# Attention with a bias behind the softmax, on one core: the preparation ahead of round 0, and the form in which the key and query parts are stored, are rebuilt

## The chip, the cores and the metric

The kernel runs on 1 core of a Trainium2 chip. The metric is the device time of one execution in microseconds (us). TensorE (PE) multiplies and loads weights (PEld), VectorE (DVE), ScalarE (ACT) and GpSimd (POOL) do the elementwise work, and SyncE (SP) issues most of the DMAs.

## The reference, cut to what matters

```python
def _L0_attn_ref(x, Wq, Wk, Wv, rel_table, gamma, beta):
    b, s, e = x.shape                       # 4, 512, 128; 16 heads of 8
    q = split_heads(x @ Wq); k = split_heads(x @ Wk); v = split_heads(x @ Wv)
    attn = softmax(jnp.einsum('bhqd,bhkd->bhqk', q, k) * e ** -0.5)
    bias = rel_table[clip(r[None, :] - r[:, None] + s - 1, 0, 2 * s - 2)]
    attn = attn + bias.reshape(-1).reshape(h, s, s)[None]
    out = jnp.einsum('bhqk,bhkd->bhqd', attn, v)      # then heads side by side
    return (out - mean) / sqrt(var + 1e-3) * gamma + beta

x = _layernorm(x + _L0_attn_ref(...))
x = _layernorm(x + _L0_ffn_ref(...))        # product keys: top 4 of 32 experts per token
```

All in float32. The bias does not depend on the batch and is added behind the softmax, so its share of the output is bias @ v.

## The kernel before

The kernel is written engine by engine, with every wait on a semaphore by hand; the order of the lines of an engine's block is its order of work. There are B = 4 batches of S = 512 tokens, H = 16 heads of D = 8 columns, in G = 4 groups of J = 4 heads, and C = 4 pieces of 128 tokens.

**Parts.** A product of float32 numbers is made in bf16: each of q and k is split into three bf16 parts (high, middle, low) whose sum is the number. Every part of q has to meet every part of k, so the stack of a head has TERMS = 72 rows (8 columns times 9 pairs of parts), and one matmul over 72 rows (96 with zeros) gives the exact scores. `parts` holds the three parts in SBUF. `write_parts` (L359) writes them to the DRAM tensor `stack_dram` [batch, q or k, head, 72, 512], each part three times; for batch 0 the first group of heads goes first. `load_slice` (L324) loads one group's 72 rows of four heads into `q_stack` and `k_stack`, 288 KB each.

**Preparation, before round 0.** `prep(b)` on PE (L1105) turns x of batch b, makes q, k and v of it. ACT (L632 to L650) copies the turned x (`x_t`), the high parts, the middle parts and v. DVE makes what is left of q and k (L819) and the low parts of batch 0 (L824); POOL makes the other low parts (L500). The bias needs the table `rel_win`, turned to `rel_t`; bias @ v of groups 0 and 1 is one product (L1321, kept by `bias_spread`), that of groups 2 and 3 is made in pieces (L1344) that ACT copies (`bias_copy`), PE turns and ACT keeps (`bias_keep`).

**Maxima.** The softmax needs the maximum of each row of scores before the exponential. PE makes the scores of 128 queries against 512 keys in one of two banks of `sm_ps`, DVE reduces them to a column of `neg_max` (L838). Maxima run 7 units ahead of the scores that use them, so 24 "early" maxima (`early_maxima`) stand between the pieces of the preparation. After the 16 maxima of a group POOL splits the column block (`split_shift`), PE turns it, ACT copies it (`shift_copy`, 0.3 us) and SP loads it into three rows of `q_stack` (`load_shift`, L335; 3 x 16 pieces of 256 bytes, from 48 partitions).

**Rounds.** Round t (0 to 4) has 16 units. A unit makes scores for four heads (`scores`), four maxima (five in the first four units of round 0), the products with v (`values`), and ACT takes four exponentials (L713). From round 1 on the feed-forward layer of the batch before lies between them. The first `scores` of round 0 waits for the shift rows of group 0 (L1168) and for all of the bias (L1362).

**SP's queue** is in order: each DMA is issued when those before it have been, and a wait blocks all behind it. `load_slice` of (t, g) waits until round t - 1 is done with group g.

## Time and profile before

| | |
|---|---|
| median of 3 runs | 312.98 us (312.96 to 313.03) |
| the profiled execution | 312.77 us, span 311.0 us |
| busy: PE, DVE, ACT, POOL | 91%, 75%, 64%, 40% of the span |
| round 0 begins (first scores) | 41.40 us from the span's start |
| moved over HBM | 12.18 MB read, 10.52 MB written |

The profile shows one execution, of 312.77 us; 1.77 us of it lie around the span. Times of instructions count from the span's start. A share of DMA is the mean busy share of 16 DMA engines: 0.75 is 12 engines at work. "A <- B" behind a row names what the engine waited for.

### The profile page before, as it was taken

What the parts mean: (1) busy time and instruction counts of PE and PEld (TensorE: products, weight loads), DVE (VectorE), ACT (ScalarE), POOL (GpSimd) and SP (SyncE); (2) the same over time, 40 slices, a digit from 0 to 9 for tenths busy, and PEclk for the clock granted to TensorE, in tenths of its full rate; (3) what the DMA queues carried; (4) which work ended last, traced back from release to release, by engine and by line L of the source; (5) the groups of instructions that cost most, each with busy time, mean ns of one, the idle gap of its engine ahead of it and who ended that gap; (6) DMA issues with size and microseconds to landing.
All of it is one profiled execution on the core that took longest, in us unless ns stands there. A gap on an engine that the chain in (4) does not pass through costs nothing.

```text
span 311.0 us, 9808 instructions
## 1 busy us (share of the span) xinstructions
PE 283.6 (91%) x4087; PEld 131.2 (42%) x4087; DVE 231.8 (75%) x516; ACT 199.1 (64%) x392; POOL 125.8 (40%) x209
## 2 busy tenths in 40 slices
PE   4878988999998989999999999999999999889991
PEld 2545232333333333343455543434555433284390
DVE  4547788988889969987798699977986952167673
ACT  2575276777676767789865667898665689902500
POOL 8393511101102751127556312297563033943133
PEclk9999999999999999999999999999999999999997
DMA  6475597359432303000403020006000000100002
GB/s 171 103 235 175 144 322 122 80 207 308 179 99 57 81 4 78 6 2 17 140 4 78 4 78 5 3 8 184 4 2 6 2 5 1 36 4 2 0 6 62
DMA packets 28265, 23.48 MB, mean 76 GB/s; under 512 B 6542, under 2 KB 26686, under 8 KB 28222
## 3 DMA queue, kind: packets, MB, share of 16 engines
q1 hardware_dynamic: 27950, 22.73, 25.9%
q8 instruction: 32, 0.52, 0.7%
q10 hardware_dynamic: 272, 0.13, 0.1%
q14 instruction: 11, 0.09, 0.1%
HBM read 12.18 MB, written 10.52 MB: 73 GB/s over the span
## 4 chain that ended last, share of the span: by engine, by line
PE 62%; DVE 15%; POOL 8%; ACT 7%; issue 4%; DMA 3%; SPq 1%; POOLq 0%; DVEq 0%
PE sm_ps L1139 13%; PE st_ps L1139 11%; PE ov_ps L1189 11%; DVE neg_max L838 9%; PE si_ps L1139 6%; PE mi_ps L1139 5%; ACT probs L713 3%; PE mi_ps L1195 2%; PE st_ps L1412 2%; POOL rstd L466 2%; PE sm_ps L1150 2%; DVE stats L877 2%; ACT w_rows L624 1%; DMA k_stack<-stack_dram 1%; PE si_ps L1213 1%
## 5 line engine op out<-in xcount | busy, mean ns | idle before, releaser
L838 DVE TENSOR_REDUCE neg_max<-sm_ps 128x1 f32<-128x512 f32 x256 | 166.0, 685 | 37.1 <-PE sm_ps L1139 30.9
L713 ACT ACTIVATE probs<-st_ps 128x512 f32<-128x512 f32 x256 | 138.3, 613 | 41.7 <-PE st_ps L1139 41.7
L1139 PE MATMUL sm_ps<-k_stack,q_stack 96*32 96x512 bf16 x928 | 91.6, 383 | 4.5 <-DVE neg_max L838 3.9
L1139 PE MATMUL st_ps<-q_stack,k_stack 128*32 128x512 bf16 x1024 | 89.0, 380 | 1.3 <-ACT bias_v L624 0.7
L1189 PE MATMUL ov_ps<-probs,v_cur 128*32 128x512 f32 x512 | 66.5, 592 | 0.0
L1139 PEld LDWEIGHTS sm_ps<-k_stack,q_stack 96*32 96x32 bf16 x928 | 24.7, 94 | 64.6 <-DVE neg_max L838 52.7
L480 POOL TENSOR_TENSOR hid<-hid,w_rows 128x512 f32<-128x512 f32 x26 | 32.9, 1281 | 36.1 <-ACT w_rows L624 36.0
L1139 PEld LDWEIGHTS st_ps<-q_stack,k_stack 128*32 128x32 bf16 x1024 | 27.5, 96 | 34.8 <-ACT probs L713 16.0
L901 DVE SCALAR_TENSOR_TENSOR hid<-tanh_sb,mi_ps 128x512 f32<-128x512 f32 x24 | 16.3, 680 | 12.0 <-ACT tanh_sb L750 12.0
L1139 PE MATMUL mi_ps<-x_t,down_sb 128*32 128x512 f32 x192 | 25.0, 592 | 0.0
L1139 PE MATMUL si_ps<-up_sb,hid 128*32 128x128 f32 x768 | 24.0, 272 | 0.0
L1139 PEld LDWEIGHTS si_ps<-up_sb,hid 128*32 128x32 f32 x768 | 21.3, 110 | 5.0 <-issue 3.5
L436 POOL CAST shift_parts<-neg_max 128x16 bf16<-128x16 f32 x16 | 3.1, 195 | 46.8 <-DVE neg_max L838 45.1
L750 ACT ACTIVATE tanh_sb<-mi_ps 128x512 f32<-128x512 f32 x24 | 14.9, 620 | 8.1 <-PE mi_ps L1139 8.1
L1189 PEld LDWEIGHTS ov_ps<-probs,v_cur 128*32 128x32 f32 x512 | 16.2, 110 | 8.5
L624 ACT ACTIVATE w_rows<-si_ps 128x512 f32<-128x512 f32 x24 | 15.6, 648 | 0.7 <-PE si_ps L1139 0.6
L452 POOL COPY v_cur<-v_all 128x128 f32<-128x128 f32 x16 | 4.5, 291 | 23.7 <-PE ov_ps L1189 23.7
L624 ACT ACTIVATE x_t<-mi_ps 128x512 f32<-128x512 f32 x4 | 2.4, 597 | 13.5 <-PE mi_ps L1195 13.5
L1139 PE MATMUL si_ps<-w_t,spread 96*32 96x512 bf16 x96 | 9.4, 382 | 1.5 <-ACT w_rows L624 1.5
L1150 PE MATMUL sm_ps<-k_stack,q_stack 96*128 96x512 bf16 x24 | 8.9, 385 | 2.0 <-DMA k_stack<-stack_dram 1.5
L461 POOL TENSOR_SCALAR veps<-mv 128x4 f32<-128x4 f32 x8 | 1.9, 235 | 18.4 <-DVE mv L886 18.4
L466 POOL TENSOR_TENSOR rstd<-veps,minus_half 128x4 f32<-128x4 f32 x8 | 8.3, 1038 | 0.2
(166 smaller groups left out, 297.3 us busy)
## 6 DMA issues: line engine op xcount, KB each, us to landing
stack_dram<-parts SPq DMA_DIRECT2D x18, 384.0 KB, 4.5
q_stack<-stack_dram SPq DMA_DIRECT2D x16, 288.0 KB
k_stack<-stack_dram SPq DMA_DIRECT2D x16, 288.0 KB
stack_dram<-parts SPq DMA_DIRECT2D x6, 288.0 KB, 4.4
x_sb<-L_attn_x SPq DMA_DIRECT2D x4, 256.0 KB, 3.9
out<-y_out SPq DMA_DIRECT2D x3, 256.0 KB, 2.3
stack_dram<-parts SPq DMA_DIRECT2D x6, 96.0 KB, 2.1
down_sb<-L_ffn_values_down SPq DMA_DIRECT2D x1, 512.0 KB, 9.0
```

Of the source, the lines that this page charges most:

```text
L466: nc.gpsimd.tensor_tensor(scale[:], v[:], minus_half[:], ALU.pow).then_inc(done, 1)
L480: nc.gpsimd.tensor_tensor(hid[:, j], hid[:, j], w_rows[:, j], ALU.mult).then_inc(weighed, 1)
L624: return nc.scalar.activation(dst, src, ACT.Copy, scale=scale)
L713: nc.scalar.activation(probs[:, u % 2, j, :], st_ps[:, score_bank(u * J + j), :], ACT.Exp, scale=SCORE_SCALE).then_inc(probs_ready, 1)
L750: nc.scalar.activation(tanh_sb[:, j % 3, :], mi_ps[:], ACT.Tanh, scale=0.5).then_inc(act_step, 1)
L838: nc.vector.tensor_reduce(neg_max[:, g % 2, col:col + 1], sm_ps[:, c % 2, :], AX.X, ALU.max, negate=True).then_inc(max_ready, 1)
L877: i = nc.vector.bn_stats(into[:, c, :], src[:, c, :])
L901: nc.vector.scalar_tensor_tensor(out=hid[:, j], in0=tanh_sb[:, j % 3, :], scalar=1.0, in1=mi_ps[:], op0=ALU.add, op1=ALU.mult).then_inc(hi ...
L1139: i = nc.tensor.matmul(dst[n * TILE:(n + 1) * TILE], weights[:, n * TILE:(n + 1) * TILE], moving, **flags)
L1150: return nc.tensor.matmul(dst, weights, moving, **flags)
L1189: i = nc.tensor.matmul(ov_ps[j * TILE:(j + 1) * TILE, :], v_cur[:, kc, g * J + j, :], probs[:, u % 2, j, :], start=(g % 2 == 0 and kc == 0 ...
L1195: return nc.tensor.transpose(dst, src, idn)
```

## The change

- The parts are stored once: `parts_dram` [batch, q or k, 24 rows, head, 512]. The load makes the 72 rows of them: its source pattern has a dimension with stride 0 and count 3. For q that dimension is the inner one (24 rows, each three times), for k it is the outer one (three times 24 rows). A row of four heads is one piece of 4 KB. A batch's write is 6 DMAs of 128 KB in place of 6 of 384 KB; batch 0's first group goes out part by part as the parts are made, and its DMAs have the four heads as outer dimension.
- x of all batches is loaded first; the weights are loaded from ACT's queue. PE turns x of batches 0 and 1 first, then those of 2 and 3. The turned x lie in `hid`, v is copied by DVE.
- The bias pieces use other PSUM banks and `tiled` maxima (four products of 32 columns) between them.
- k of the last batch is made after maximum 18, its q after maximum 23; their parts are made within round 0, at units 0 and 3.
- The load of `rel_win`, `hasher` and `keys` moves behind batch 0's first writes.

```diff
-        stack_dram = nc.dram_tensor("stack_dram", [B, 2, H, D * PARTS * PARTS, S], BF16, kind="Internal").ap()
+        parts_dram = nc.dram_tensor("parts_dram", [B, 2, PARTS * D, H, S], BF16, kind="Internal").ap()
...
+        def turned_bank(b):
+
+            return [st_ps[:, 0, :], ov_ps[:, :], sm_ps[:, 0, :], sm_ps[:, 1, :]][b]
+
+        def qk_bank(b, a):
+
+            return [(st_ps[:, 1, :], st_ps[:, 2, :]), (mi_ps[:, :], si_ps[:, :])][b % 2][a]
...
@@ -328,9 +341,9 @@
                     sp.wait_ge(scores_ready, (t - 1) * (J * U) + J * C * (g + 1))
                     apart(sp)
                 for a, stack in enumerate((q_stack, k_stack)):
-                    src = stack_dram[t, a, g * J:(g + 1) * J]
-                    sp.dma_start(stack[0:TERMS, g * J:(g + 1) * J, :], src.rearrange("h r s -> r h s")) \
-                      .then_inc(stack_loaded[g], 16)
+                    rows = [[H * S, PARTS * D], [0, PARTS]] if a == 0 else [[0, PARTS], [H * S, PARTS * D]]
+                    src = bass.AP(parts_dram.tensor, (t * 2 + a) * PARTS * D * H * S + g * J * S, rows + [[1, J * S]])
...
 
             sp.sem_inc(y_stored, 1)
 
+            def load_x(b):
+                sp.dma_start(x_sb[:, b], x[b].rearrange("(c p) e -> p c e", p=P)).then_inc(x_loaded[b], 16)
+
             for b in range(B):
-                sp.dma_start(x_sb[:, b], x[b].rearrange("(c p) e -> p c e", p=P)).then_inc(x_loaded[b], 16)
-                if b == 0:
-                    for dst, src in ((wq_sb, w_q), (wk_sb, w_k), (wv_sb, w_v)):
-                        sp.dma_start(dst[:], src).then_inc(proj_loaded, 16)
+                load_x(b)
             sp.dma_start(beta_sb[:], bass.AP(beta.tensor, 0, [[0, P], [1, E]])).then_inc(beta_loaded, 16)
 
             sp.dma_start(rel_dram[0:LAST + 1, :], rel_table).then_inc(rel_written, 16)
             sp.dma_start(rel_dram[LAST + 1:, :],
                          bass.AP(rel_table.tensor, LAST * H, [[0, NWIN + P // H - LAST - 1], [1, H]])).then_inc(rel_written, 16)
-            sp.wait_ge(rel_written, 32)
-            sp.dma_start(rel_win[:], bass.AP(rel_dram.tensor, 0, [[H, P], [H * P, NWIN // P], [1, P]])) \
-              .then_inc(rel_loaded, 16)
-            sp.dma_start(hasher_sb[:], hasher_w).then_inc(keys_loaded, 16)
-            sp.dma_start(keys_sb[:], keys).then_inc(keys_loaded, 16)
+            def load_tables():
+
+                sp.wait_ge(rel_written, 32)
+                sp.dma_start(rel_win[:], bass.AP(rel_dram.tensor, 0, [[H, P], [H * P, NWIN // P], [1, P]])) \
+                  .then_inc(rel_loaded, 16)
+                sp.dma_start(hasher_sb[:], hasher_w).then_inc(keys_loaded, 16)
+                sp.dma_start(keys_sb[:], keys).then_inc(keys_loaded, 16)
 
             def write_parts(b, heads, written):
 
-                for a in range(2):
-
-                    sp.wait_ge(*((first_split, a + 1) if b == 0 else (low_made, split_count(b, a))))
-                    rows = stack_dram[b, a, heads].rearrange("h (d i j) s -> (h d) i j s", i=PARTS, j=PARTS)
-                    for n in range(PARTS):
-                        dst = rows[:, :, n, :] if a == 0 else rows[:, n, :, :]
-                        sp.dma_start(dst, parts[heads.start * D:heads.stop * D, b, a]).then_inc(written, 16)
+                for i in range(PARTS):
+                    for a in range(2):
+                        if b:
+                            sp.wait_ge(low_made, split_count(b, a))
+                        else:
+                            sp.wait_ge(*((high_made, a + 1), (first_mid, a + 1), (first_split, a + 1))[i])
+                        rows = parts_dram[b, a, :, heads].rearrange("(i d) h s -> i h d s" if a == 0 else
+                                                                   "(d i) h s -> i h d s", i=PARTS)
+                        sp.dma_start(rows[i], parts[heads.start * D:heads.stop * D, b, a, i]).then_inc(written, 16)
 
 
             write_parts(0, slice(0, J), first_written)
+            load_tables()
             sp.wait_ge(first_written, 2 * PARTS * 16)
 
             sp.wait_ge(stack_set, 1)
...
+            pool.wait_ge(beta_loaded, 16)
+            add_beta(0)
+            add_beta(1)
+            low_parts(1)
+            low_parts(2)
+            pool.wait_ge(v_copied, B)
             for g in range(G):
...
+            add_beta(3)
+            split_shift(0, 0)
+            for n, a in enumerate((1, 0)):
+                pool.wait_ge(last_copied, n + 1)
+                nc.gpsimd.tensor_sub(resid[:, 1, a], resid[:, 1, a], parts[:, B - 1, a, 0, :]).then_inc(last_resid, 1)
...
+                if is0(t):
+                    low_parts(B - 1)
...
+            def x_copy(b):
+
+                act.wait_ge(x_turned, b + 1)
+                copy(x_t(b), turned_bank(b)).then_inc(xt_copied, 1)
+
+            def high_parts(b):
+
+                for a in range(2):
+                    act.wait_ge(qk_made, 2 * b + a + 1)
+                    copy(parts[:, b, a, 0, :], qk_bank(b, a)).then_inc(high_made, 1)
+
+            for dst, src, loaded in ((wq_sb, w_q, proj_loaded[0]), (wk_sb, w_k, proj_loaded[1]), (wv_sb, w_v, proj_loaded[2])):
+                nc.scalar.dma_start(dst[:], src).then_inc(loaded, 16)
+            x_copy(0)
+            x_copy(1)
+            high_parts(0)
+            middle_parts(0)
+            x_copy(2)
+            x_copy(3)
+            high_parts(1)
+            middle_parts(1)
+            high_parts(2)
...
+            def last_parts(a):
+                act.wait_ge(qk_made, 2 * B - a)
+                copy(parts[:, B - 1, a, 0, :], qk_bank(B - 1, a)).then_inc(high_made, 1)
+                act.wait_ge(low_made, split_count(1, a))
+                copy(resid[:, 1, a], qk_bank(B - 1, a)).then_inc(last_copied, 1)
+
+            bias_keep(CG)
+            last_parts(1)
             bias_keep(G - 1)
...
+                    if u == 0 and is0(t):
+                        last_parts(0)
+                    if u == 3 and is0(t):
+                        middle_parts(B - 1)
+                        act.wait_ge(rows_loaded, 32)
...
-                            .then_inc(first_split, 1)
-
-            for b in range(B - 1):
-                resids(b)
+                    dve.wait_ge(high_made, 2 * b + a + 1)
+                    nc.vector.tensor_sub(resid[:, b % 2, a], qk_bank(b, a), parts[:, b, a, 0, :]).then_inc(resid_made, 1)
+
+            def v_copy(b):
+
+                dve.wait_ge(v_made, b + 1)
+                nc.vector.tensor_copy(v_all[:, :, :, b, :].rearrange("p c h d -> p (c h) d"),
+                                      v_bank(b).rearrange("p (n d) -> p n d", d=D)).then_inc(v_copied, 1)
+
+            resids(0)
+            for a in range(2):
+                dve.wait_ge(first_mid, a + 1)
+                nc.vector.tensor_sub(parts[:, 0, a, 2, :], resid[:, 0, a], parts[:, 0, a, 1, :]).then_inc(first_split, 1)
+            v_copy(0)
+            resids(1)
+            v_copy(1)
+            resids(2)
+            v_copy(2)
+            v_copy(3)
 
             def maximum(t, pos, c):
 
...
-                prep(b)
+                        maximum_scores(0, *early.pop(0), product=product)
...
+            turn_x(0)
+            turn_x(1)
+            pe.wait_ge(proj_loaded[0], 16)
+            make_qk(0, 0)
+            pe.wait_ge(proj_loaded[1], 16)
+            make_qk(0, 1)
+            turn_x(2)
+            turn_x(3)
+            pe.wait_ge(proj_loaded[2], 16)
+            make_v(0)
+            make_qk(1, 0)
+            make_qk(1, 1)
+            make_v(1)
+            make_qk(2, 0)
+            make_qk(2, 1)
+            make_v(2)
+            pe.wait_ge(high_made, 4)
+            pe.wait_ge(resid_made, 4)
+            pe.wait_ge(rel_loaded, 16)
+            for n in range(NWIN // P):
+                i = turn(mi_ps[:, n * P:(n + 1) * P], rel_win[:, n, :], ident[:])
+            i.then_inc(table_mm, 1)
+            make_v(3)
+            pe.wait_ge(keys_loaded, 32)
+            turn(si_ps[0:PD, 0:NE], keys_sb[:], ident[0:NE, 0:NE]).then_inc(table_mm, 1)
+            pe.wait_ge(xt_copied, B)
             early_maxima(2)
-
...
-            early_maxima(1)
-            turn(st_ps[0:PD, 1, 0:NE], keys_sb[:], ident[0:NE, 0:NE]).then_inc(table_mm, 1)
-            early_maxima(1)
             pe.wait_ge(table_copied, 2)
...
+            pe.wait_ge(resid_made, 6)
             for kc in range(C):
                 i = nc.tensor.matmul(st_ps[:, 2, 0:CG * J * B * D], rel_t[:, LAST:LAST + P],
                                      v_all[:, kc, 0:CG * J].rearrange("p h b d -> p (h b d)"),
                                      start=(kc == 0), stop=(kc == C - 1))
-                early_maxima(1 + kc % 2)
+                early_maxima(1)
...
+                    bias_product(g, kc)
+                    early_maxima(1, product=tiled)
+            early_maxima(EARLY, J * C + 2, tiled)
+            pe.wait_ge(table_copied, 3)
+            make_qk(B - 1, 1)
+            pe.wait_ge(consts_made, 8)
+            pe.wait_ge(shift_split, 1)
+            turn(mi_bf[:, 0:P], shift_parts[:].rearrange("p i n -> p (i n)"), ident_bf[:]).then_inc(misc_ready, 1)
+            early_maxima(1, EARLY)
+            bias_turn(CG)
+            early_maxima(2, EARLY)
             bias_turn(G - 1)
+            early_maxima(2, EARLY)
+            pe.wait_ge(misc_done, 1)
+            make_qk(B - 1, 0)
             early_maxima(EARLY, EARLY)
-            pe.wait_ge(bias_kept, G - CG + 1)
...
+                    if is0(t) and u == 0:
+                        pe.wait_ge(bias_copied, G - CG)
```

On SP, what stands from the tables to the first loads and the second writes, before (the names are those of the text above; "4x8x512" are the sizes of the pattern written, its outer one first):

```order
L354 DMA rel_win<-rel_dram 128x4x128 [waits rel_written]
L356 DMA hasher_sb<-L_ffn_hasher_w 32x128
L357 DMA keys_sb<-L_ffn_keys 32x32
L367 DMA stack_dram<-parts 96x1x512 [waits first_split]
L367 DMA stack_dram<-parts 96x1x512 x2
L367 DMA stack_dram<-parts 32x1536 [waits first_split]
L367 DMA stack_dram<-parts 32x1536 x2
L332 DMA q_stack<-stack_dram 72x4x512 [waits rows_cleared,stack_set,first_written]
L332 DMA k_stack<-stack_dram 72x4x512
L367 DMA stack_dram<-parts 288x1x512 [waits first_split]
```

and now:

```order
L384 DMA parts_dram<-parts 4x8x512 [waits high_made] x2
L384 DMA parts_dram<-parts 4x8x512 [waits first_mid] x2
L384 DMA parts_dram<-parts 4x8x512 [waits first_split] x2
L369 DMA rel_win<-rel_dram 128x4x128 [waits rel_written]
L371 DMA hasher_sb<-L_ffn_hasher_w 32x128
L372 DMA keys_sb<-L_ffn_keys 32x32
L346 DMA q_stack<-parts_dram 72x1x2048 [waits rows_cleared,stack_set,first_written]
L346 DMA k_stack<-parts_dram 72x1x2048
L384 DMA parts_dram<-parts 12x8x512 [waits high_made] x2
```

The first six writes wait for one part each instead of for all three, the tables stand between them and the loads, and a load has pieces of 2048 elements instead of 512.

On PE, from the sixteenth early maximum (L1150 before) to the first scores of round 0, before:

```order
L1195 MATMUL mi_ps<-ident_bf,shift_parts 128x128 [waits shift_split,consts_made,last_copied]
L1344 MATMUL st_ps<-rel_t,v_all 32x288 x4
L1150 MATMUL sm_ps<-k_stack,q_stack 128x512 [waits max_ready]
...
L1195 MATMUL st_ps<-ident,bias_t 128x128 [waits bias_kept,bias_copied]
L1195 MATMUL st_ps<-ident,bias_t 128x128 x3
L1150 MATMUL sm_ps<-k_stack,q_stack 128x512 [waits max_ready] x2
L1195 MATMUL st_ps<-ident,bias_t 128x128 [waits bias_copied]
L1195 MATMUL st_ps<-ident,bias_t 128x128 x3
L1139 MATMUL st_ps<-q_stack,k_stack 32x512 [waits shift_loaded0,bias_kept]
```

and now (L1159 makes k and q of the last batch):

```order
L1159 MATMUL si_ps<-hid,wk_sb 128x512 [waits high_made,resid_made,xt_copied,table_copied]
L1232 MATMUL mi_ps<-ident_bf,shift_parts 128x128 [waits shift_split,consts_made]
L1185 MATMUL sm_ps<-k_stack,q_stack 128x512 [waits max_ready]
L1232 MATMUL ov_ps<-ident,bias_t 128x128 [waits v_copied,bias_copied]
...
L1232 MATMUL ov_ps<-ident,bias_t 128x128 [waits bias_kept,bias_copied]
...
L1159 MATMUL mi_ps<-hid,wq_sb 128x512 [waits high_made,resid_made,xt_copied,misc_done]
L1185 MATMUL sm_ps<-k_stack,q_stack 128x512 [waits max_ready]
L1174 MATMUL st_ps<-q_stack,k_stack 32x512 [waits shift_loaded0]
```

The bias products are all ahead of the turned shift now, and the first scores wait for the shift rows alone.

## Rows read from the trace of the kernel before

**Rows 1.** Chain of waits, 0 to 60 us: start, length, what it ran on.

```profile
14.57 1.89 DMA stack_dram<-parts
16.48 0.31 SPq L332
16.83 4.27 DMA k_stack<-stack_dram
...
39.14 0.70 DVE neg_max L838
...
40.75 0.61 ACT bias_v L624
41.40 0.62 PE st_ps L1139 x8
```

**Rows 2.** Timeline of SP's issues: start, length of the issue, line, DMA, count.

```profile
10.01 0.39 SPq L354 DMA_DIRECT2D rel_win<-rel_dram  x1
...
11.46 3.55 SPq L367 DMA_DIRECT2D stack_dram<-parts  x6
...
17.30 6.17 SPq L367 DMA_DIRECT2D stack_dram<-parts  x6
26.53 0.31 SPq L332 DMA_DIRECT2D q_stack<-stack_dram  x1
...
28.74 0.43 SPq L332 DMA_DIRECT2D k_stack<-stack_dram  x1
35.66 0.85 SPq L338 DMA_DIRECT2D q_stack<-shift_rows  x1
```

**Rows 3.** Groups of DVE's instructions, 21 to 41.4 us: early maxima.

```profile
L838 DVE TENSOR_REDUCE neg_max<-sm_ps 128x1 f32<-128x512 f32 x24 | 15.8, 689 | 5.7 <-PE sm_ps L1150 5.5
```

**Rows 4.** DMA share and GB/s by stretch (last two columns; start:end first).

```profile
5.00:6.50 1.50, 1.07 (x2) 0.58 (x3) 0.11 (x1) 0.29 (x1) 1.44 (x2) 1.00 1.09 326
28.00:36.00 8.00, 7.08 (x60) 2.85 (x58) 6.52 (x10) 2.91 (x6) 1.87 (x5) 1.00 0.81 213
69.50:71.50 2.00, 1.98 (x28) 0.69 (x24) 1.96 (x4) 1.75 (x4) 0.80 (x4) 1.00 1.01 391
104.00:105.00 1.00, 1.00 (x20) 0.35 (x16) 1.00 (x3) 1.00 (x3) 0.92 (x2) 1.00 0.00 0
116.40:116.70 0.30, 0.30 (x8) 0.09 (x4) 0.30 (x1) 0.30 (x2) 0.00 (x0) 1.00 0.17 37
```

**Rows 5.** Timelines of PE and DVE: x of batch 0 turned, its q, its low parts.

```profile
3.57 1.08 PE L1116 MATMUL st_ps<-ident,x_sb 128*128 128x128 f32 x4 [3.57 <-DMA x_sb<-L_attn_x]
5.43 2.05 PE L1125 MATMUL st_ps<-x_t,wq_sb 128*128 128x512 f32 x2 [0.78 <-ACT x_t L624]
...
10.46 1.47 DVE L824 TENSOR_TENSOR parts<-resid,parts 128x512 bf16<-128x512 f32 x2
```

**Rows 6.** SP's timeline: loads of group 2 and of group 0, batches 1 and 2.

```profile
88.48 0.38 SPq L332 DMA_DIRECT2D q_stack<-stack_dram  x1
...
104.24 0.31 SPq L332 DMA_DIRECT2D q_stack<-stack_dram  x1
```

**Rows 7.** Timeline of PE before round 0: last bias product, maximum, second turn.

```profile
37.14 0.69 PE L1344 MATMUL st_ps<-rel_t,v_all 128*32 128x288 f32 x8
37.77 0.39 PE L1150 MATMUL sm_ps<-k_stack,q_stack 96*128 96x512 bf16 x1
38.09 0.69 PE L1344 MATMUL st_ps<-rel_t,v_all 128*32 128x288 f32 x8
...
40.11 0.60 PE L1195 MATMUL st_ps<-ident,bias_t 128*128 128x128 f32 x4
```

**Rows 8.** Groups of ACT's instructions, 41.4 to 56 us: exponentials of round 0.

```profile
L713 ACT ACTIVATE probs<-st_ps 128x512 f32<-128x512 f32 x18 | 9.8, 598 | 4.4 <-PE st_ps L1139 4.4
```

**Rows 9.** PE's timeline: the first maximum that uses that group.

```profile
94.71 0.39 PE L1139 MATMUL sm_ps<-k_stack,q_stack 96*32 96x512 bf16 x4
```

More of the change, by code:

```diff
@@ new lines, in turn_x, with make_qk @@
+                for c in range(C):
+                    i = nc.tensor.transpose(turned_bank(b)[:, c * P:(c + 1) * P], x_sb[:, b, c, :], ident[:])
+                i.then_inc(x_turned, 1)
+            def make_qk(b, a):
+                pe.wait_ge(xt_copied, b + 1)
+                if b >= 2:
+                    pe.wait_ge(high_made, 2 * (b - 2) + a + 1)
+                    pe.wait_ge(resid_made, 2 * (b - 2) + a + 1)
+                nc.tensor.matmul(qk_bank(b, a), (wq_sb, wk_sb)[a][:], x_t(b), start=True, stop=True).then_inc(qk_made, 1)
@@ L1178, in values @@
                 if kc == 0:
+                    if is0(t) and g == 0:
+                        pe.wait_ge(bias_kept, G - CG + 1)
                     pe.wait_ge(v_ready, t * G + g + 1)
@@ L1318, in _, with bias_turn, bias_product @@
-            pe.wait_ge(table_copied, 3)
+                        maximum_scores(0, *early.pop(0), product=product)
+            def bias_turn(g):
+                pe.wait_ge(bias_copied, g - CG + 1)
+                pe.wait_ge(v_copied, B) if g == CG else pe.wait_ge(bias_kept, g - CG + 1)
+                for c in range(C):
+                    i = turn(bias_banks(g)[1][:, c * P:(c + 1) * P], bias_t[:, g % 2, c * P:(c + 1) * P], ident[:])
+                i.then_inc(bias_turned, 1)
+            def bias_product(g, kc):
+                n = constant_from((g + 1) * J - 1) + 1
+                for j in range(J):
+                    h = g * J + j
+                    window = bass.AP(rel_t, S - 1 - HPB * h + (P // H) * kc, [[pitch, P], [HPB, n], [-1, HPB]])
+                    i = nc.tensor.matmul(bias_banks(g)[0][j * TILE:(j + 1) * TILE, 0:n * HPB],
+                                         v_all[:, kc, h].rearrange("p b d -> p (b d)"), window,
+                                         start=(kc == 0), stop=(kc == C - 1))
+                if kc == C - 1:
+                    i.then_inc(bias_mm, 1)
@@ L1323, in _ @@
                                      start=(kc == 0), stop=(kc == C - 1))
-                early_maxima(1 + kc % 2)
+                early_maxima(1)
             i.then_inc(bias_mm, 1)
-            def bias_turn(g):
-                pe.wait_ge(bias_copied, g - CG + 1)
-                pe.wait_ge(bias_kept, g - CG + 1) if g == CG else pe.wait_ge(bias_copied, 2)
-                for c in range(C):
-                    i = turn(bias_banks(g)[1][:, c * P:(c + 1) * P], bias_t[:, g % 2, c * P:(c + 1) * P], ident[:])
-                i.then_inc(bias_turned, 1)
```

152 lines of the change are left out of this document (40 added, 112 removed).

## The prediction

> **What bounds the kernel now.** I read the chain of waits first, because the change touches only the first 41 us and the first round. It shows what decides when the first early maximum can run: batch 0's parts are written to DRAM (landed at 14.57 + 1.89 = 16.46), loaded back (issued from 16.48, landed at 21.10), and only then can PE and DVE begin their 24 early maxima [rows 1]. Round 0 starts at 41.40, 20.3 us later. SP's timeline shows what stands in the queue on the way: the six first writes, all issued after the low parts, in 3.55 us, then six larger ones, and at 26.53 the loads of groups 1 to 3 [rows 2]. In those 20.3 us DVE reduces for 15.8 us and is idle for 5.7 (the stretch of the row begins a little earlier), nearly all of it waiting for PE [rows 3]; PE lies between with the rest of batch 3, the tables and the bias pieces. The last wait is for ACT's last kept piece of the bias [rows 1]. From 41.40 on a unit of round 0 has five maxima of 0.69 us and the rounds are bound by PE and DVE together; the change leaves that work as it is. So what it is worth is how much earlier round 0 can start, less what it pushes into the rounds.
>
> **The load, the part that decides.** A load of one group is 288 KB for q and 288 KB for k, 295 kB each. Two facts about how many of the 16 DMA engines a load gets can be seen. The stack loads, with 72 rows as outer dimension on both sides, run at a share of 0.81 with 213 GB/s, which is 12 or 13 engines of 16, while the large writes with 128 partitions fill the share to 1.01 [rows 4]. The load of the shift rows, with 3 rows on the writing side and 48 partitions on the reading side, shows a share of 0.17 over 0.30 us: three engines for just under that time, though the reading side alone would feed all 16 [rows 4]. So the side with the smaller outer dimension decides, and 72 gives 12. The changed k load has 72 rows outside on the SBUF side, but its source has 3 copies outside and 24 rows inside. By the pattern of the shift rows it gets three engines. The q load has 24 outside and 72 rows on the other side, both divisible by 12: it keeps twelve.
>
> The Trainium skill ("DMA: Bandwidth & Descriptors", section "Why a DMA increments its semaphore by 16 and not by 1") states it so: the number of engines is the largest one up to 16 that divides the outer dimension of both patterns, and the lowest-numbered engines are taken. Both rows agree with the first half, 12 for 72 and 3 for 3 against 48; which engines they are no row names. It speaks against this change; without it (k on twelve engines) the sum would be that of the first rival.
>
> Rate of one engine: writes 391 / (1.01 x 16) = 24.2 GB/s, x loads in pieces of 512 bytes 326 / (1.09 x 16) = 18.7, stack loads in pieces of 1 KB with twelve at once 213 / (0.81 x 16) = 16.4 [rows 4]. No row shows pieces of 4 KB. I take 24.2, since the pieces are the largest of all and the writes have the largest pieces of the rows (up to 3 KB); 16.4 stays as the low end. On each of the three engines a pair of loads is then 98.3 kB of k and 24.6 kB of q: 123 / 24.2 = **5.1 us** (7.5 at the low end). Over twelve engines 590 kB at 213 GB/s is 2.8 us.
>
> **The sum, in order of time.**
> 1. *Parts of batch 0.* PE now turns x of two batches ahead of q. The second takes 1.08 as the first does [rows 5]; 0.78 of it fills a gap in which PE waited for ACT's copy [rows 5], so all behind it is 0.3 late. The low parts end at 11.93 before (10.46 + 1.47), at about 12.2 now. The weights come on ACT's queue beside x; q waited for ACT's copy last, not for them: 0.
> 2. *First writes.* Before, six issues of 0.59 follow the low parts' start. Now four of them are out before, and one is issued behind the last low part; the tables' three issues (10.01 to 11.46, 1.45 us [rows 2]) follow it, in the time the write takes to land. With 1.9 for landing [rows 1] and some issues in line the q load goes out at 14.4 in place of 16.48: -2.1.
> 3. *First load.* No byte moves until 0.8 after the issue (104.24, nothing until 105 [rows 4, 6]). 14.4 + 0.8 + 5.1 + 0.2 to land = 20.5, against 21.10.
> 4. *Second writes.* Twelve heads outside, so twelve engines, 49 kB on each: 2.0 us. On the three engines they lie behind k, so they end at 20.3 + 2.0 = 22.3 and have landed at 22.8; the loads of groups 1 to 3 are issued from there, in place of 26.53.
> 5. *Three loads and the shift rows.* 22.8 + 0.8 + 3 x 5.1 = 38.9. The shift rows use three engines as well. I take them for the same three, so that they lie behind those loads: + 0.3 + 0.2 gives 39.4. (With others, step 6 would decide, at 38.) The first scores wait for them.
> 6. *Maxima and bias.* From 20.5, with DVE never idle, the 24 maxima end at 36.3; with all idle time and PE work of before they would end with the stretch of 20.3, at 40.8. Batch 3's v and the turned table are out of the stretch. The last four bias products still take PE 0.95 a step (37.14 to 38.09) where DVE needs 0.69 [rows 7], though tiled maxima can shorten the 0.32 behind a maximum; and the second turn (40.11), whose keeping ended last before, has two maxima behind it now. I take 38. So step 5 ends last, and round 0 begins at 39.4 to 40.0, I say 39.7: **-1.7**.
> 7. *Moved into round 0.* Four ACT copies of 0.6 for the last batch. ACT is idle for 4.4 of 14.6 us there [rows 8], but they come in pairs ahead of an exponential, and the unit's slack is about 1.0. Bounds 0 and 2.4; I take **+0.3**, near the slack. PE's wait for `bias_copied` and the waits in `values` ask for work that is 10 us old: 0. POOL's low parts of batch 3 wait in front of a split that is not due before unit 4: 0. If that cover went, a unit would slip by up to 2.3.
> 8. *Later loads.* Every group is loaded at 5.1 instead of 2.8. The tightest is group 2 of batch 1: issued at 88.48 [rows 6], needed at 94.71 [rows 9]. All moves up alike; 88.48 + 0.8 + 5.1 + 0.2 = 94.6: **0**, with 0.1 to spare. The others have 5 us or more between issue and use. The lighter writes (3.1 MB in place of 9.4) free the queue, but nothing waited for them: 0.
>
> The sum is -1.4 on the profiled execution's 312.77, which gives **311.4**; that execution is 0.2 below the median of the runs, so against 312.98 it is -0.5%. A measurement of this kernel can tell about 0.2% (0.6 us) from nothing.
>
> **Rivals.**
> *The k load keeps twelve engines.* For it: no row has a source dimension of stride 0 outside with a wide destination; against it: the shift rows. Then the first load lands at 14.4 + 0.8 + 2.8 + 0.2 = 18.2, the maxima path of step 6 decides (17.5 behind it), and round 0 starts at 35.7: -5.7 + 0.3, **307.4**. Chance 0.17.
> *The k load is slower still: slower than before.* The place is the same queue of three engines. Four loads lie in series ahead of the shift rows, and a fifth step (group 2 of batch 1) has 0.1 to spare. Each 0.1 us per pair costs 0.4 at the start and 0.1 there. It decides from 5.4 us per pair, 22.6 GB/s per engine: only 7% below my value. For it: both kinds of loads from DRAM in the rows run at 16.4 and 18.7. Against it: smaller pieces, more engines at once. Halfway to the low end, 20.3 GB/s, a pair takes 6.05: 4 x 0.95 + 0.9 - 1.4 = +3.3, **316.1**; at the low end 7.5 and 323. Chance 0.23.
> *Nothing to measure.* A rate near 22.6, or ACT's copies at 1.5 in place of 0.3: **312.8**. Chance 0.15.
>
> **How the numbers follow.** The forecast has 0.45, of which 0.40 lies beyond 0.2%. Faster 0.40 + 0.17 = 0.57, same 0.15 + 0.04 = 0.19, slower 0.24. The forecast's own range, from the steps' roundings (0.6 each for steps 5 to 7), is 310.0 to 313.0. To hold 8 in 10 it has to reach the first rival, 307, and the half-way case of the second, 316; the low end of the rate is left out.
>
> **What would show it.** Right: the k loads run at a DMA share near 0.2 and about 73 GB/s; the first maximum is at 20 to 21 us; PE waits for the DMA of the shift rows ahead of round 0, at 39 to 40, with DVE idle before it for over 1 us. The first rival: a share near 0.8 in the loads, first maximum near 18.3, and no wait for a DMA at the start. The second: first maximum beyond 21.5, start of round 0 beyond 42, and a wait for `k_stack` at unit 1 of round 1. Wrong in another way: round 0 starts early and its units are longer than 3.5 us, with ACT ahead of PE's waits.

## The result and the profile after

| | before | changed |
|---|---|---|
| median of the runs | 313.00 us (4 runs, 312.96 to 313.11) | **319.53 us** (4 runs, 319.39 to 322.24) |
| ratio to before, 95% interval | 1 | 1.0228 (1.0174 to 1.0282) |
| profiled execution, and its span | 312.77, 311.0 | 319.39, 316.7 |
| mean granted clock of TensorE | 0.994 | 0.977 |
| first early maximum on PE | 21.14 | 23.32 |
| start of round 0 (first scores) | 41.40 | 44.42 |
| first `w_rows` copy on ACT, in round 1 | 137.08 | 142.76 |

The change makes the kernel slower, outside the range given. The last three lines of the table tell where: 2.2 us at the first maximum, 3.0 at the start of round 0, 5.7 in round 1, and then the distance stays (the last output store is issued at 307.61 and at 313.39). The chain of waits of the changed kernel names the two places (start, length, what ran):

```profile
12.12 0.50 SPq L384
12.66 0.58 SPq L384
13.79 0.50 SPq L371
14.88 0.84 SPq L346
15.77 7.41 DMA k_stack<-parts_dram
23.32 1.01 PE sm_ps L1185 x2
...
38.08 6.30 DMA q_stack<-shift_rows
...
92.20 7.46 DMA k_stack<-parts_dram
100.54 1.24 PE ov_ps L1226 x8
```

Against [rows 1] the q load goes out 1.6 us earlier (14.88 for 16.48), but the k load takes 7.41 us in place of 4.27. The load of the shift rows, a 12 KB transfer, is now in the chain for 6.30 us, and group 2 of batch 1 for 7.46. The waits of PE in the changed kernel over the whole span (us in total, times, the longest):

```profile
PE st_ps L1174 <- DMA q_stack<-shift_rows: 2.9, 1, 2.9
PE sm_ps L1174 <- DMA k_stack<-parts_dram: 2.0, 1, 2.0
```

and, in the first 44 us, `PE sm_ps L1185 <- DMA k_stack<-parts_dram` for 5.5 us. The windows of the changed kernel (its time, then the busy time of PE, PEld, DVE, ACT and POOL, the granted clock, the DMA share, GB/s), where the k loads of groups 1 to 3 are alone, and in round 1:

```profile
34.00:40.00 6.00, 5.43 (x51) 2.24 (x39) 5.27 (x9) 2.86 (x7) 0.83 (x4) 1.00 0.19 75
...
98.00:99.00 1.00, 0.00 (x0) 0.00 (x0) 0.00 (x0) 0.65 (x2) 0.00 (x0) 1.00 0.19 78
99.00:100.00 1.00, 0.29 (x8) 0.19 (x12) 0.00 (x0) 0.00 (x0) 0.00 (x0) 1.00 0.20 82
100.00:101.00 1.00, 1.00 (x20) 0.38 (x16) 0.84 (x2) 0.60 (x1) 0.00 (x0) 0.95 0.18 74
101.00:102.00 1.00, 1.00 (x11) 0.18 (x8) 0.97 (x4) 0.00 (x0) 0.28 (x1) 0.50 0.19 78
102.00:103.00 1.00, 1.00 (x16) 0.44 (x12) 0.93 (x2) 0.32 (x1) 1.00 (x2) 0.50 0.20 82
103.00:104.00 1.00, 1.00 (x16) 0.35 (x10) 0.89 (x3) 0.74 (x2) 0.67 (x4) 0.50 0.24 78
104.00:106.00 2.00, 2.00 (x32) 0.72 (x24) 1.80 (x6) 1.22 (x3) 0.08 (x1) 0.92 0.00 0
```

A share of 0.19 is three of 16 engines, and 75 GB/s over three is 25 each: the load runs as the prediction had it. Two things it did not have: a load starts moving bytes later, behind a longer issue, and PE, idle for 2.0 us in round 1, works at the lower level of its clock (0.50, which is 1.2 GHz) for over three us, from 1.2 us behind its return.

### The profile page after: what moved, and what is told of

Its sections match the earlier page's. It is cut to its first block, busy times and chain, and to the rows that moved or that the text cites. A ratio compares the mean times of both kernels' runs of the same rounds, so it can differ in the third digit from the quotient of the medians.

```text
span 316.7 us, 9874 instructions
## 1 busy us (share of the span) xinstructions
PE 285.2 (90%) x4117; PEld 132.9 (42%) x4117; DVE 234.4 (74%) x520; ACT 196.9 (62%) x388; POOL 125.3 (40%) x209
## 4 chain that ended last, share of the span: by engine, by line
PE 59%; DVE 14%; POOL 8%; DMA 8%; ACT 6%; issue 3%; SPq 2%; POOLq 0%; DVEq 0%
PE sm_ps L1174 13%; PE st_ps L1174 11%; PE ov_ps L1226 11%; DVE neg_max L878 9%; PE si_ps L1174 6%; PE mi_ps L1174 5%; DMA k_stack<-parts_dram 5%; ACT probs L742 3%; DMA q_stack<-shift_rows 2%; PE st_ps L1467 2%; POOL rstd L484 2%; PE mi_ps L1232 2%; ACT w_rows L649 1%; PE si_ps L1250 1%; DVE stats L917 1%
## 5 line engine op out<-in xcount | busy, mean ns | idle before, releaser
L1174 PE MATMUL sm_ps<-k_stack,q_stack 96*32 96x512 bf16 x968 | 96.3, 386 | 6.0 <-DVE neg_max L878 3.4
L1174 PEld LDWEIGHTS sm_ps<-k_stack,q_stack 96*32 96x32 bf16 x968 | 25.9, 95 | 68.0 <-DVE neg_max L878 53.0
L1174 PEld LDWEIGHTS st_ps<-q_stack,k_stack 128*32 128x32 bf16 x1024 | 27.8, 97 | 38.3 <-ACT probs L742 16.6
L1185 PE MATMUL sm_ps<-k_stack,q_stack 96*128 96x512 bf16 x14 | 6.4, 487 | 5.6 <-DMA k_stack<-parts_dram 5.5
L518 POOL TENSOR_TENSOR parts<-resid,parts 128x512 bf16<-128x512 f32 x6 | 6.8, 1156 | 10.8 <-ACT parts L649 10.8
L479 POOL TENSOR_SCALAR veps<-mv 128x4 f32<-128x4 f32 x8 | 1.9, 235 | 19.1 <-DVE mv L926 19.1
```

Of the source, the lines that this page charges most:

```text
L518: nc.gpsimd.tensor_sub(parts[:, b, a, 2, :], resid[:, b % 2, a], parts[:, b, a, 1, :]) \
L1174: i = nc.tensor.matmul(dst[n * TILE:(n + 1) * TILE], weights[:, n * TILE:(n + 1) * TILE], moving, **flags)
L1185: return nc.tensor.matmul(dst, weights, moving, **flags)
```

## The experiments

All times below are medians; before, on the same chips, had 313.04 to 313.20. Starts and waits are read from one profiled execution each. The edits are shown shortened; where k has more DMAs, the count that PE waits for rises with them. The first ones test the k load, its neighbour in the queue, and the clock.

**Three DMAs of 24 rows for k.**

```diff
-rows = [[0, PARTS], [H * S, PARTS * D]]
-sp.dma_start(stack[0:TERMS, g * J:(g + 1) * J, :], src)
+rows = [[H * S, PARTS * D]]            # k alone; q's load stays
+for i in range(PARTS):
+    sp.dma_start(stack[i * PARTS * D:(i + 1) * PARTS * D, g * J:(g + 1) * J, :], src)
```

> The change as it is, but every k load is issued as three DMAs of 24 rows, one for each copy, so that both sides have 24 as their outer dimension; all else is unchanged (the count that PE waits for is 64 a group). Theory A (the k load runs on three engines because its outer dimension is 3, and that is what makes the kernel slower): a group's pair lands about 3 us after its last issue, the DMA share beside it is near 0.7, the first maximum runs at 19.5 to 20.5 (23.32 in the change: one load of 2.8 us in place of 6.4, less 1.5 for two more issues), PE no longer waits for shift rows, round 0 starts at 37.5 to 39 and the wait for k in round 1 is gone: 307 to 309 us. Theory B (the longer issues on SP, 0.7 to 0.85 us in place of 0.4, and the queue behind the writes make it slower): two issues more for each group make it worse, first maximum later than 22, round 0 at 42 or later, 317 or more.

Measured: **309.91 us**, 0.9891 of before (0.9858 to 0.9924). First maximum 21.22, round 0 at 38.92, no wait for shift rows, none for k in round 1. While groups 1 to 3 are loaded its windows show (columns as above)

```profile
28.00:30.00 2.00, 2.00 (x48) 0.92 (x42) 2.00 (x4) 0.68 (x2) 0.25 (x1) 1.00 0.77 197
```

Theory A holds: the same bytes over twelve engines, with two more issues for each group, are 9.6 us faster than the change. 197 GB/s at a share of 0.77 is 16 GB/s for each of twelve engines, where each of the three moved 25, both with pieces of 4 KB. The first maximum is 0.7 later than the latest I expected (below).

**A control: two DMAs for k, each still with 3 copies outside.**

```diff
-sp.dma_start(stack[0:TERMS, g * J:(g + 1) * J, :], src)
+for n in range(1 if a == 0 else 2):
+    cols = J if a == 0 else J // 2
+    h = g * J + n * cols
+    src = bass.AP(parts_dram.tensor, (t * 2 + a) * PARTS * D * H * S + h * S, rows + [[1, cols * S]])
+    sp.dma_start(stack[0:TERMS, h:h + cols, :], src)
```

> A control for the run with three DMAs of 24 rows: every k load is split too, but into two halves of its columns (2 KB pieces), each still with a source of 3 copies outside and 24 rows inside. Theory A (the outer dimension of 3 takes each DMA to the same three engines): nothing is gained, a DMA share of 0.17 to 0.20 beside k alone, first maximum at 23.2 to 24.5, round 0 at 44 to 46.5, 319 to 323 us. Rival (a second DMA finds other engines, so that splitting alone is what helped): share near 0.35, first maximum at 20.5 to 21.5, round 0 at 40 or earlier, under 313 us.

Measured: **322.13 us**, 1.0251 (1.0194 to 1.0308). First maximum 24.35, round 0 at 45.90 behind a wait of 3.41 us for the shift rows, and where k loads are alone

```profile
36.00:38.00 2.00, 1.60 (x17) 0.53 (x10) 1.99 (x4) 1.03 (x2) 0.57 (x3) 1.00 0.19 74
```

in the same columns: still three engines. Splitting alone only adds issues; what helped was 24 as the outer dimension. The stride of 0 by itself is not it: q's load has one inside, with 24 outside, and while it runs (16.5 to 17.5 in the change) the share is 0.74, with 254 GB/s. The Trainium skill ("DMA: Bandwidth & Descriptors", the section named in the prediction) says that each DMA takes the lowest-numbered engines; by that rule two loads of three engines share three, and this run agrees.

**Shift rows ahead of group 3.**

```diff
-for g in range(1, G):     load_slice(0, g)
-load_shift(0, 0)
+for g in range(1, G - 1): load_slice(0, g)
+load_shift(0, 0)
+load_slice(0, G - 1)
```

> The change as it is, but the first shift rows are loaded ahead of group 3 in place of behind it; the k loads stay on their engines. Theory A1 (in the start it is the place of the shift rows behind the third pair on the three engines that costs): they land at about 39, PE's wait of 2.9 us for them goes, and round 0 starts when the early maxima end, at 41.6 to 42.0 in place of 44.42; the wait for k in round 1 stays: 316.5 to 317.0 us. Rival (the shift rows had other engines, or other work is as late): they land at 43 or later and the time is 319 to 320.

Measured: **317.61 us**, 1.0132 (1.0100 to 1.0164): 1.9 faster than the change, where 2.5 to 3 was expected. Round 0 starts at 42.20 and no longer waits for shift rows. Up to the first maximum the edit changes nothing, yet this profile has it at 24.37, 1.05 later than the change's: q's issue comes 0.3 later, and k takes 8.29 us from its issue to PE's return (16.08 to 24.37) in place of 7.55. So the start in this profile understates the gain; the mechanism is shown by the wait that is gone. The shift rows had stood behind the third pair on the same engines.

**The same, with six unread products on PE in the first wait.**

```diff
 pe.wait_ge(xt_copied, B)
+for _ in range(6):
+    nc.tensor.matmul(sm_ps[:, 0, :], wq_sb[:], x_t(0), start=True, stop=True)
 early_maxima(2)
```

> As the one before, and PE runs six float32 products of 512 columns, whose results nobody reads, while it would wait for the first load. Theory C (PE's idle 5.5 us take its clock to half until 28.5, and this costs time too): the granted clock stays at 1.0 from 22 to 29, the first 6 us of maxima and bias pieces take 3, the early maxima end at 39.5 to 40 and round 0 starts at 40: 314.5 to 315.5. Rival (DVE's 0.69 us a maximum bounds that stretch anyway): round 0 starts at 41.5 or later, within 0.5 us of the one before.

Measured: **315.97 us**, 1.0072 (1.0044 to 1.0100), round 0 at 41.87. The median fell by 1.6, the start by only 0.33, and the clock was not held: it fell at 26.3 and stayed at 0.50 until 29.7, after stretches (22 to 26) in which PE was busy for 2.8 us of 4. The six products ended 0.77 us before PE went on at 24.16. Part of the median's gain may lie elsewhere: without the products the clock fell once more, from 97.9 to 101.3, behind a wait of 1.78 us for k in round 1; with them that wait is 1.70 and the clock stays at 1.00. The run does not decide; the next ones do.

**Three DMAs, four unread products.** The same edit with `range(4)`, on the version with three DMAs.

> The k load as three DMAs of 24 rows, and four float32 products of 512 columns that nobody reads on PE while it would wait for the first load. Theory C (the idle PE loses its clock, and DVE then waits for scores in 24 to 28): granted clock 1.0 from 21 to 28, DVE's gaps of 0.25, 0.59 and 0.59 (several in a row) close, round 0 starts at 37.5 to 38.0 in place of 38.92, 308.5 to 309.2 us. Rival (as in the run before: the fall only comes later and something else bounds): 309.6 to 310.2.

The windows of the kernel with three DMAs alone (the clock is the column ahead of the DMA share):

```profile
22.00:24.00 2.00, 1.55 (x7) 0.96 (x7) 2.00 (x4) 0.20 (x1) 2.00 (x4) 0.89 0.34 98
24.00:26.00 2.00, 2.00 (x6) 1.35 (x6) 1.17 (x3) 0.00 (x0) 1.74 (x3) 0.50 0.14 49
26.00:28.00 2.00, 2.00 (x18) 1.17 (x19) 1.34 (x3) 0.53 (x1) 1.92 (x2) 0.75 0.81 227
```

and of the one with the four products as well:

```profile
22.00:24.00 2.00, 1.55 (x8) 0.98 (x8) 2.00 (x4) 0.20 (x1) 2.00 (x2) 1.00 0.26 78
24.00:26.00 2.00, 2.00 (x11) 1.28 (x9) 2.00 (x4) 0.00 (x0) 1.74 (x3) 1.00 0.36 123
26.00:28.00 2.00, 2.00 (x45) 1.05 (x44) 2.00 (x4) 1.02 (x1) 1.79 (x2) 1.00 0.76 180
```

DVE is now busy for all of 22 to 28, where it had waited for 1.5 us, and round 0 starts at 37.45 in place of 38.92: theory C holds for the place. But the time is **309.82 us**, 0.9894 (0.9859 to 0.9930), no better as far as these runs can tell: 0.82 us come back as a wait for k in round 1, and only 0.7 of the 1.5 reaches `w_rows` (133.92 for 134.58).

**The same, group 3 of rounds 1 to 3 loaded only when group 2 has landed.**

```diff
 if not is0(t):
+    sp.wait_ge(stack_loaded[G - 2], 64 * (t + 1))
     load_slice(t, G - 1)
```

> Three DMAs of 24 rows for k, four unread products on PE in the first wait, and group 3 of the later batches loaded only when group 2 has landed. The run without the last part started round 0 at 37.45 (1.47 earlier) but lost 0.82 again in round 1, waiting for k of group 2. Theory G (the two pairs share the engines): that wait is gone, 308.8 to 309.3 us. Rival (group 2 is late because it is asked for early, not because of group 3): the wait stays at 0.7 to 0.9, 309.6 to 310.0 us.

Measured: **309.00 us**, 0.9864 (0.9839 to 0.9890), the fastest here and 4.1 below before. Its interval overlaps with those of the two versions before it, so that it is faster than they are is not shown. Round 0 starts at 36.78, but the edit does not touch the start; this profile was 0.65 early already at the first load's issue (14.24 for 14.89). The wait is 0.34, so both theories have a part: from the issue of group 2's q to the end of PE's wait it is 6.33 us (84.09 to 90.42) in place of 6.80 (84.76 to 91.56).

**The same wait in the changed kernel** (count 32 in place of 64).

> The change as it is, but in rounds 1 to 3 SP issues the loads of group 3 only when group 2 has landed. Theory G (two pairs on the same three engines share them, which is why group 2 of batch 1 landed 8.3 us after its first issue): it lands 0.7 to 1.2 us earlier, the wait for k in round 1 falls from 2.0 to about 1 us, 318.3 to 318.9 us. Rival E (an engine works its queue in order): the wait stays, 319.3 to 319.7 us; group 3 is needed over 10 us later in both.

Measured: 319.96 us, 1.0202 (1.0161 to 1.0243), nothing gained. From q's issue to the end of the wait: 7.98 us (91.87 to 99.85), 8.40 in the change (91.31 to 99.71). But the two versions with the shift rows early, where the next pair follows as in the change, show 8.20 and 8.11. Sharing with the next pair costs 0.1 to 0.4 by these profiles, not the 0.7 to 1.2 I had given it; the rest of the lateness is the load's own. This profile also lost the clock from 45.6 to 49.0, behind PE's wait of 2.70 for the shift rows, which the change's did not behind a wait of 2.90; so its total tells little of the edit.

**Second writes held back until the first load has landed.**

```diff
 load_slice(0, 0)
+sp.wait_ge(stack_loaded[0], 32)
 write_parts(0, slice(J, H), parts_written[0])
```

> The change as it is, but SP issues the six second writes only when the first load has landed. It tells why the first k load took 7.41 us from its issue where 5.1 was worked out. Theory D (writes that are issued behind a load share its three engines with it and slow it): with nothing behind it the k load lands 5.5 to 5.8 us after its issue, and the first maximum runs at 21.3 to 21.8 in place of 23.32. Rival E (the engines take the queue in order, and the load itself is slower than I worked out): 7.2 to 7.5 us, first maximum at 23.2 to 23.5. In both the later loads are issued later, so the whole is no faster: 319 to 323 us.

Measured: 324.64 us (two runs), 1.0362 (1.0311 to 1.0413). The load is issued at 15.93 and PE goes on at 23.00: 7.07 us, near rival E's value and 0.5 under the change's 7.55 (15.77 to 23.32). Three more profiles that are the same up to there have 7.72 (the last one above) and 8.29 and 8.17 (shift rows early). So the writes behind it cost 0.5 in the change and up to 1.2, if one profile without them can be trusted that far. Its windows of half a microsecond give the rest:

```profile
16.00:16.50 0.50, 0.50 (x6) 0.41 (x5) 0.45 (x2) 0.26 (x1) 0.50 (x1) 1.00 0.02 3
16.50:17.00 0.50, 0.50 (x6) 0.50 (x6) 0.50 (x2) 0.00 (x0) 0.25 (x1) 1.00 0.47 82
17.00:17.50 0.50, 0.50 (x7) 0.50 (x6) 0.50 (x1) 0.39 (x1) 0.00 (x0) 1.00 0.70 287
17.50:18.00 0.50, 0.50 (x6) 0.36 (x4) 0.08 (x1) 0.21 (x1) 0.00 (x0) 1.00 0.58 221
18.00:18.50 0.50, 0.10 (x1) 0.00 (x0) 0.49 (x1) 0.36 (x2) 0.00 (x0) 1.00 0.18 49
18.50:19.00 0.50, 0.00 (x0) 0.00 (x0) 0.20 (x1) 0.50 (x2) 0.08 (x1) 1.00 0.20 49
19.00:19.50 0.50, 0.00 (x0) 0.00 (x0) 0.00 (x0) 0.36 (x1) 0.50 (x1) 1.00 0.08 33
19.50:20.00 0.50, 0.00 (x0) 0.00 (x0) 0.00 (x0) 0.00 (x0) 0.50 (x1) 1.00 0.19 74
```

The q load was issued at 15.05, and its bytes move from 16.5: 1.5 us, not the 0.8 I had read from [rows 4, 6]. From 18.0 to 19.5 k runs at 33 to 49 GB/s, then at 74 (once 90) until 22.5. Why it starts slowly no run tells.

**The new order with the old storage** (nine stored rows, written nine times behind the low parts, 1 KB pieces, 72 rows outside).

```diff
-src = bass.AP(parts_dram.tensor, (t * 2 + a) * PARTS * D * H * S + g * J * S, rows + [[1, J * S]])
+src = parts_dram[t, a, g * J:(g + 1) * J].rearrange("h r s -> r h s")
```

> The change with one part undone: parts are stored in the old layout (nine rows for each row of a head, written nine times behind the low parts) and loaded from 72 rows with 1 KB pieces; the new order of the preparation, the bias pieces and the last batch stay. Theory A (only the k load's three engines make it slower): the first k load takes 4.3 to 5 us, the first maximum runs at 21.5 to 22.3, round 0 starts at 39.5 to 40.5 and round 1 has no wait for k: 311 to 312.5 us. Rival (the new order of the preparation is itself slower): round 0 at 42 or later, over 313.5.

Measured: **312.10 us**, 0.9967 (0.9950 to 0.9984). First maximum 20.98, earlier than I expected, round 0 at 39.71, no wait for k in round 1. The new order of the preparation alone is worth 0.9 us, with a clock of 0.50 from 21.5 to 28.3 in it. Its start is 1.7 earlier than before's; 0.9 of that goes in round 0, where PE waits 0.89 us, until 54.09, for the next shift rows. SP issues them at 50.12, behind the heavier writes and a table load that ends at 50.07; with three DMAs for k they go out at 48.14 and nothing waits.

**The old order with the new storage** (parts written once, as high, middle and low parts are made; q with stride 0 inside; k as three DMAs).

> The kernel before with the storage alone changed: parts stored once, q loaded with a stride of 0 inside, k as three DMAs of 24 rows; preparation, tables and bias pieces as before. Theory H (the storage pays only with the new order: here SP still issues the tables until 11.46 and all six first writes behind them, and a pair of loads takes 2.2 us of issues in place of 0.8): q goes out at about 16.2, the first maximum runs at 21.3 to 22, round 0 starts at 41.5 to 42.2: 312.8 to 313.8 us. Rival (the lighter writes and larger pieces are worth the 2.2 us by which the change with three DMAs beat the change with the old storage): first maximum at 19.5 to 20.5, round 0 at 39.5 to 40, 310.5 to 311.5 us.

Measured: **316.28 us**, 1.0087 (1.0054 to 1.0120), slower than either expectation. The q load goes out at 16.86, the first maximum runs at 22.30 and round 0 starts at 44.24: 1.2 us lost at the load, 2.8 at the start. In round 1 PE waits another 1.11 us for k, and `w_rows` is 4.1 late (141.18 for 137.08). And the same with three unread products on PE in that wait:

> The kernel before with the storage changed (k as three DMAs), which took 316.28 us, and three float32 products that nobody reads on PE while it would wait for the first load. Theory C (there the load was 1.2 us later than before, and the other 1.7 us of the start came from the clock at half speed until 26.8): with the clock held at 1.0 round 0 starts at 42.4 to 42.9 in place of 44.24, 314.3 to 315.0 us. Rival (the later load alone, through a longer PE stretch behind it, costs all of the 2.8 us): round 0 at 43.8 to 44.5, 315.8 to 316.5.

Measured: **315.17 us**, 1.0055 (1.0032 to 1.0078). This is the cleanest price of the clock, since the first maximum runs at 22.30 and at 22.31. The windows behind it without the products

```profile
24.00:25.00 1.00, 1.00 (x3) 0.59 (x2) 0.03 (x2) 0.43 (x1) 0.22 (x1) 0.50 0.46 136
25.00:26.00 1.00, 1.00 (x2) 0.24 (x2) 0.68 (x1) 0.65 (x2) 0.27 (x1) 0.50 0.03 8
```

and with them

```profile
24.00:25.00 1.00, 1.00 (x4) 0.40 (x4) 0.71 (x2) 1.00 (x3) 0.06 (x2) 1.00 0.45 134
25.00:26.00 1.00, 1.00 (x10) 0.88 (x9) 0.69 (x1) 0.97 (x3) 1.00 (x1) 1.00 0.01 4
```

Round 0 starts at 42.57 in place of 44.24: 1.67 us, as theory C had it (the low clock ended at 26.3 there, not at 26.8). The median falls by 1.1, less than that, and the two intervals overlap; it is the pair of profiles that shows the price.

**Weights on SP's queue between the loads of x**, on the version with three DMAs.

```diff
-nc.scalar.dma_start(dst[:], src).then_inc(loaded, 16)
+sp.dma_start(dst[:], src).then_inc(proj_loaded[b], 16)      # behind load_x(b), b = 0, 1, 2
```

> The k load as three DMAs of 24 rows, and the three weight loads on SP's queue between the loads of x, in place of ACT's. Theory F (x of batch 0 lands 0.6 us later, because the weights move at the same time): the first turn of x starts at 3.6 as before, everything up to round 0 is 0.5 to 0.6 earlier, 309.2 to 309.5 us. Rival (x of batch 1 or the weights then land later than they are asked for): the first q product at 6.3 or later, no gain, 309.8 to 310.5.

Measured: 311.07 us, 0.9928 (0.9904 to 0.9953), 1.2 slower than without by the medians, though the intervals overlap. x of batch 0 is turned at 3.69 instead of 4.17, but batch 1 only at 5.42 instead of 5.16, and q's first product starts at 6.32 instead of 6.07: the rival's case, and slower than the rival's 309.8 to 310.5. In this profile the clock was at 0.50 from 20.8 to 27.6, without the edit from 23.6 to 27.0, which can be part of it.

## Why the prediction was wrong

The direction of the second rival came true, by its mechanism (the queue of three engines) and at its signs: first maximum beyond 21.5, round 0 beyond 42, a wait for `k_stack` in round 1. But the size it hung on, the rate of an engine, came out as forecast, and by luck: I took 24.2 GB/s because the pieces are the largest, and with the same 4 KB pieces twelve engines moved 16 each once groups 1 to 3 were under way (above), no more than with the 1 KB pieces before. (The rival's breakeven of 5.4 us a pair is 22.8 GB/s, not 22.6.) What failed is a term beside the rate: the time from a load's issue to PE's return, put at 6.1 us and measured at 8.4, at the first load and again at group 2 of batch 1. Step by step:

1. *Parts of batch 0.* The low parts end at 12.11 (12.2 predicted). x lands 0.7 late behind the weights, which I had at nothing; since q waits for the second turn in any case, moving the weights away gave nothing back.
2. *First writes.* q's issue at 14.88, 14.4 predicted. The last write is issued 12.66 to 13.24, and the tables' issues end at 14.75, 0.13 ahead of q's. The profile lists no wait for the writes' landing there: the tables set it, not the landing. Missing: 0.5.
3. **First load, the step that failed first.** Predicted 0.8 + 5.1 + 0.2 = 6.1 us from q's issue; measured 8.4 (14.88 to 23.32). Three engines and 25 GB/s each were right. The terms that were too small: bytes move 1.5 us after the issue begins, not 0.8, with an issue of 0.84 us where [rows 2]'s loads took 0.31 to 0.43; a slow first stretch of k (with the writes held back, three windows of 0.5 us at 49, 49 and 33 GB/s in place of 74) costs 0.6; the writes behind it 0.5. The 0.5 left are not traced.
4. *Second writes.* Landed at 25.2, 22.8 predicted. They were issued until 21.3 (4.77 us) and ran beside k's load. They landed 2.0 behind it (23.2), close to the 2.3 worked out; the lateness is that of steps 2 and 3.
5. **Three loads and the shift rows: the step that set the end, as predicted, but 5.0 us later** (44.42 for 39.4). 2.5 of that is step 4's; the other 2.5 is the distance from the first issue (25.27) to the landing, 19.1 us where 0.8 + 15.3 + 0.5 = 16.6 was worked out. Of it 0.7 is the later start of the bytes (26.8). Against the 2.0 that 39.4 would have gained, the 5.0 are the 3.0 lost at the start.
6. *Maxima and bias.* Predicted 38; PE is ready for round 0 at 41.52 (44.42 less its wait of 2.90), 18.2 us behind the first maximum. I had costed the stretch at 17.5 and the clock at nothing: PE is idle for 5.5 us, and the granted clock is 0.50 from 22.4 to 29.2. It was hidden behind step 5 in the change, and decided once the loads were quick (1.5 us with three DMAs).
7. *Moved into round 0.* Predicted 0.3: nothing. With three DMAs round 0 starts 2.48 before before's, and `w_rows` comes 2.50 before. (Step 8's "nothing waited" for the lighter writes held only for the old start: with the new order and the old storage PE waits 0.89 us in round 0.)
8. **Group 2 of batch 1, the same failure: predicted 0, with 0.1 to spare; measured 2.7.** PE's wait of 2.0, and the rest, by my reading, in the three us at the lower clock behind it. From q's issue to PE's next product 8.4 us, not 6.1: the same start (0.7), up to 0.4 for sharing with group 3's pair, and the rest the load's own, not traced further.

Of step 5, the windows of the changed kernel's last stretch, in which PE comes to wait for the shift rows, are

```profile
40.00:42.00 2.00, 1.53 (x5) 0.49 (x4) 1.73 (x3) 0.51 (x2) 1.15 (x1) 1.00 0.32 110
42.00:43.00 1.00, 0.00 (x0) 0.00 (x0) 0.26 (x1) 0.00 (x0) 0.00 (x0) 1.00 0.88 297
43.00:44.00 1.00, 0.00 (x0) 0.00 (x0) 0.00 (x0) 0.00 (x0) 0.00 (x0) 1.00 0.95 285
```

More moves here than k's three engines can carry. The load of gamma (issued at 38.90) and batch 1's writes (from 39.84) run beside the last pair and the shift rows, and the prediction had them at nothing. By an estimate from the windows, 1540 of the three pairs' 1770 kB had moved at 40.0; the other 230 at 74 GB/s would end at 43.1, and the rows landed at 44.4. That these writes delay the rows was not tested.

So the sum of -1.4 became +3.0 at the start and +2.7 in round 1, with 0.9 more outside the span in the profiled run (0.2 to 0.9 in its other runs; unexplained). The first rival's 307.4 was tested by the version with three DMAs: 309.9. That rival's sum, too, had nothing for the later start of a load and the clock (1.5), and nothing for two more issues a group. The later start of 0.7 alone turns the forecast's sign: it comes in ahead of the first load, ahead of the three loads and, less the 0.1 to spare, at group 2, together 2.0 against -1.4, or +0.6 by the forecast's own sum. No row ahead of the result showed the start of a load with a stride of 0; I had taken it from loads of the old layout.

## What to carry to other kernels

Look at the outermost dimension of both patterns before a DMA is made from a replicating source. Put the stride of 0 inside (24 rows, 3 copies: twelve engines), or issue one DMA for each copy; outside (3 copies, 24 rows) it takes three engines here, and everything behind it on those engines, even 12 KB of shift rows, waits. When work is moved out of a wait to make something earlier, the wait becomes idle time of PE, and its clock may have to be paid for in the stretch behind it (1.5 and 1.7 us in the two pairs of profiles here): price the stretch at half speed, or leave PE something to do until the data lands.

## What the runs showed of the hardware

- *Three engines.* A source of 3 copies outside ran at 74 to 78 GB/s and a share of 0.19 to 0.20, whether one DMA or two were in flight. The Trainium skill has this too ("DMA: Bandwidth & Descriptors", "Rules for kernel authors", the row on using all 16 engines: a leading zero-stride broadcast of c copies confines a DMA to at most c of them), and the trace agrees with c = 3.
- *Rate of an engine.* 25 GB/s with three at work, 16 with twelve (197 GB/s at a share of 0.77, three DMAs for k, 28 to 30), both with 4 KB pieces; 16.4 with twelve and 1 KB pieces [rows 4]. Only the first q load of the change was faster on twelve: 254 GB/s at 0.74, 21 each.
- *Issue time.* With 4 KB pieces and a stride of 0 an issue took SP 0.70 to 0.92 us, for 24 rows without it 0.45, in the old layout 0.29 to 0.43 for the same 288 KB. The halves of k, 2 KB pieces with a stride of 0, took 0.7 each too for half of the bytes. The long issues have the stride of 0 in common; 72 rows of 4 KB without it were not tried.
- *The clock.* PE idle for 1.55 us ahead of the first maximum in before was followed by a granted clock of 1.00. Idle for 2.0 (round 1 of the change), 2.1 (old storage), 2.6, 2.9 and 5.5 us was followed by 0.50, which began between 0.9 us ahead of PE's return and 2.4 us behind it, and went on for 3 to 7 us. But the length of the last wait does not settle it: 2.90 us ahead of round 0 in the change was followed by 1.00, 2.70 in the same place of the version with the same wait (count 32) by 0.50, and so was 0.77 behind the six products. With unread products in the wait the start came 1.5 and 1.7 us earlier.
